# Three attentions of a 2,048-token block rebuilt: two float32r parts instead of three bf16 ones, scores and maxima on two halves of the rows, maxima over 1,024 keys, outputs kept by token, and the values weighed for two key tiles at a time

## The reference, cut to what is computed

```python
x = x + _L0_attn_a_ref(_layernorm(x), ...)        # token mixer
x = x + _L0_ffn_ref(_layernorm(x), ...)           # "F"
x = x + _L0_attn_b_ref(_layernorm(x), ...)        # "L", causal
x = x + _L0_ffn_ref(_layernorm(x), ...)           # "H", same weights as F

# inside _L0_ffn_ref: full attention, 16 heads of 8 channels
h = _layernorm(x, ln1_g, ln1_b)
q, k, v = h @ Wq, h @ Wk, h @ Wv                  # (1, 2048, 16, 8) each
scores = einsum('bqhd,bkhd->bhqk', q, k) / sqrt(8)
x = x + einsum('bhqk,bkhd->bqhd', softmax(scores), v) @ Wo
... layer norm, 8 experts, top 2 ...

# inside _L0_attn_b_ref: the same shape with a causal mask; the kernel
# multiplies the small latent matrices out first, so that q, k, v are
# again 2048 x 16 x 8 and no output projection is left
attn = where(causal, attn, -inf); attn = softmax(attn)
```

## Time and profile before

| | us |
|---|---|
| median of 3 runs | 3383.09 (3382.2 to 3384.76) |
| span of the profiled execution | 3382.5 |
| TensorE busy | 3032.9 (90%) |
| TensorE weight loads | 1205.9 (36%) |
| VectorE busy | 2225.2 (66%) |
| ScalarE busy | 1668.8 (49%) |
| GpSimd busy | 168.7 (5%) |
| mean granted TensorE clock, of full speed | 0.915 |

### The profile page before, as it was taken

One profiled execution on the slowest core, in us unless ns is written; L12 is line 12 of the kernel. 1 busy time (PEld: TensorE's weight loads), 2 busy tenths in 40 slices (PEclk: granted clock), 3 DMA queues, 4 the chain that ended last, 5 costly groups with the idle time before them and its releaser, 6 DMA issues. The chain is left out here.

```text
span 3382.5 us, 48839 instructions
## 1 busy us (share of the span) xinstructions
PE 3032.9 (90%) x14997; PEld 1205.9 (36%) x14997; DVE 2225.2 (66%) x4191; ACT 1668.8 (49%) x2007; POOL 168.7 (5%) x88
## 2 busy tenths in 40 slices
PE   6788859999999997997799999958999999998998
PEld 2787732222222223443233333322222222222443
DVE  5444459988889893223667666647989888894322
ACT  4212123666666665433255555531666666666333
POOL 1222220000000000001100000011000000000000
PEclk9888866999999997998699999975999999999899
DMA  1000010110011011120111111111010000110211
GB/s 37 1 0 0 0 61 11 29 29 19 27 29 29 17 30 32 69 69 12 59 32 39 30 30 41 30 32 59 15 30 29 29 19 28 29 29 21 76 56 31
DMA packets 75059, 105.46 MB, mean 31 GB/s; under 512 B 17334, under 2 KB 48016, under 8 KB 72433
## 3 DMA queue, kind: packets, MB, share of 16 engines
q1 hardware_dynamic: 71755, 100.97, 9.8%
q10 hardware_dynamic: 3104, 1.94, 0.2%
HBM read 68.72 MB, written 20.55 MB: 26 GB/s over the span
## 5 line engine op out<-in xcount | busy, mean ns | idle before, releaser
L466 DVE TENSOR_REDUCE Hmaxes<-Hm 128x1 f32<-128x512 f32 x1044 | 658.2, 685 | 95.6 <-PE Hm L392 95.0
L466 DVE TENSOR_REDUCE Fmaxes<-Fm 128x1 f32<-128x512 f32 x1044 | 658.1, 685 | 95.5 <-PE Fm L392 95.1
L447 ACT ACTIVATE Hprob<-Hs 128x1024 f32<-128x1024 f32 x512 | 498.5, 1021 | 242.3 <-PE Hs L357 240.7
L447 ACT ACTIVATE Fprob<-Fs 128x1024 f32<-128x1024 f32 x512 | 498.5, 1021 | 242.1 <-PE Fs L357 240.6
L466 DVE TENSOR_REDUCE Lmaxes<-Lm 128x1 f32<-128x512 f32 (+3 forms) x664 | 373.1, 605 | 179.0 <-PE Lm L392 105.3
L447 ACT ACTIVATE Lprob<-Ls 128x1024 f32<-128x1024 f32 (+7 forms) x384 | 293.1, 776 | 268.5 <-PE Ls L360 144.8
L392 PE MATMUL Hm<-Hka,Hqa 99*128 99x512 bf16 x1044 | 381.6, 404 | 27.4 <-DMA Hvh<-Hvstack 11.5
L392 PE MATMUL Fm<-Fka,Fqa 99*128 99x512 bf16 x1044 | 381.4, 404 | 26.8 <-DMA Fvh<-Fvstack 11.0
L357 PE MATMUL Fs<-Fqa,Fka 99*128 99x512 bf16 x1024 | 308.3, 385 | 1.6 <-ACT Fprob L447 1.2
L357 PE MATMUL Hs<-Hqa,Hka 99*128 99x512 bf16 x1024 | 308.2, 384 | 1.6 <-ACT Hprob L447 1.2
L374 PE MATMUL Ho<-Hprob,Hvh 128*32 128x512 f32 x2048 | 276.3, 612 | 0.6 <-ACT Hprob L447 0.6
(11 more groups left out here) (428 smaller groups left out, 2883.7 us busy)
## 6 DMA issues: line engine op xcount, KB each, us to landing
FEwb<-FE_weights SPq DMA_DIRECT2D x8, 1024.0 KB, 5.9
HEwb<-HE_weights SPq DMA_DIRECT2D x8, 1024.0 KB, 5.3
Fqa<-F_qparts SPq DMA_DIRECT2D x51, 96.0 KB
Fka<-F_kparts SPq DMA_DIRECT2D x51, 96.0 KB
Lqa<-L_qparts SPq DMA_DIRECT2D x51, 96.0 KB
Lka<-L_kparts SPq DMA_DIRECT2D x51, 96.0 KB
Hqa<-H_qparts SPq DMA_DIRECT2D x51, 96.0 KB
Hka<-H_kparts SPq DMA_DIRECT2D x51, 96.0 KB
```

Of the source, the lines that this page charges most:

```text
L447: nc.scalar.activation(prob[:, kt % PSLOTS, q0:q1], sps[SLOT_OF[kt, half]][:, q0 - half * 1024:1024], ACT.Exp, scale=SCALE).then_inc(expd, 1)
L466: nc.vector.reduce_max(maxes[:, qt, kb:kb + 1], src[:, 0:n], AX.X).then_inc(max_free, 1)
```

## The change

**Parts.** Queries and keys are split in two parts of float32r (`PARTS = 2`), with one copy and one subtraction. The combinations are now 4 x 8 = 32 rows, and two rows for the maximum (`KROWS = 34`). Each head's rows are loaded twice, at rows 0 to 33 for the scores and from row 64 on for the maxima (`LOW = 64`, 33 rows), so that the two kinds of product use different row halves of TensorE. Two slots instead of three.

**Maxima.** An item covers 1,024 keys: two matmuls into a pair of banks and one reduction. There are 32 a head in F and H and 24 in L, and two pairs of banks. In L the diagonal is masked by VectorE in the same operation (`tensor_tensor_reduce` with the constant `later`), and no longer by matmuls. Splitting the maxima and copying the head's values into place are on GpSimd (two instructions for the split, one for the values).

**Scores.** Each block of 512 columns has a bank of its own in a ring of three; its exponential follows at once, over 512 columns instead of 1,024. The ring also takes the turned maxima and the turned output. In L GpSimd zeroes the upper triangle of the diagonal 128x128 of the weights (`affine_select`), and blocks start at the first query of the tile.

**Weighing.** `weigh` is called after the scores of each even key tile, for the two tiles before it, one behind the other.

**The output.** TensorE transposes the copied bank in four pieces (`deliver`), ScalarE gathers it into `heads`, tokens on the partitions, and VectorE divides once for 15 heads and once for the last (`scale_heads`). The way through memory is gone. `project_tokens` transposes the result and projects it; L needs one addition (`add_tokens`).

**Loops.** TensorE, SP and GpSimd loop over two heads at a time (`Fori(1, 7)`), VectorE and ScalarE over one. The memory rows of zeros, the bf16 identity and the bf16 masks are gone. The rest of the program is not changed.

```diff
-PARTS = 3
-MROW = 96
+PARTS = 2
+MROW = PARTS * PARTS * DH
 KROWS = MROW + PARTS
+LOW = 64
+LROWS = MROW + 1
-SLOTS = 3
-MSLOTS = 3
-EARLY_FULL, EARLY_CAUSAL = 20, 24
+EARLY_FULL, EARLY_CAUSAL = 8, 9
+TURN_FULL, TURN_CAUSAL = 13, 11
...
-    MAXES = [(qt, kb, min(BANK, (qt + 1) * P - kb * BANK) if causal else BANK)
-             for qt in range(NT) for kb in range(NB) if not causal or kb * BANK <= qt * P]
+    MAXES = [(qt, half, min(2 * BANK, keys(qt) - 2 * BANK * half))
+             for qt in range(NT) for half in range(2) if keys(qt) > 2 * BANK * half]
...
-    cost = lambda j: 250 if j == "turn" else 60 + MAXES[j][2]
-    done = np.cumsum([cost(j) for _, j in stream])
+    stream = [(1, j) for j in range(EARLY, NM)] + [(2, j) for j in range(EARLY)]
+    done = np.cumsum([120 + MAXES[j][2] for _, j in stream])
...
+            sps = [ctx.enter_context(nc.psum_tensor(f"{name}s{i}", [P, BANK], F32)) for i in range(3)]
+            mps = [ctx.enter_context(nc.psum_tensor(f"{name}m{i}", [P, 2 * BANK], F32)) for i in range(2)]
+            ops = ctx.enter_context(nc.psum_tensor(name + "o", [P, BANK], F32))
...
+                        last = nc.tensor.matmul(mps[j % 2][:, n * BANK:n * BANK + w],
+                                                qa[LOW:LOW + LROWS, s, qt * P:(qt + 1) * P],
+                                                ka[LOW:LOW + LROWS, s, k0:k0 + w], start=True, stop=True)
...
+                        pe.wait_ge(expd, entry(h, kt, n) + 1)
+                        nc.tensor.matmul(seat(kt, n)[:, 0:q1 - q0], ka[0:KROWS, s, kt * P:(kt + 1) * P],
+                                         qa[0:KROWS, s, q0:q1], start=True, stop=True).then_inc(scored, 1)
...
+                            for k in range(high):
+                                for ahead, j, n in low[round(len(low) * k / high):round(len(low) * (k + 1) / high)]:
+                                    maxima(h + ahead, i + (u + ahead) // 2, (u + ahead) % 2, j, n)
+                                score(h, i, u, kt, k)
+                            for back in (2, 1):
+                                if kt % 2 == 0 and kt > 0:
+                                    weigh(h, u, kt - back)
+                                elif kt == 0 and not first:
+                                    weigh(h - 1, 1 - u, NT - back)
+                            if kt == OUT_AFTER:
+                                deliver(h, source=ident if first else None)
+                            if kt == TURN_AT:
+                                turn(turn_entry(h), TURN_SEAT, h + 2 if rest else h + 1)
...
+                            for n, (q0, q1) in enumerate(blocks(kt)):
+                                act.wait_ge(scored, entry(h, kt, n) + 1)
+                                nc.scalar.activation(prob[:, kt % PSLOTS, q0:q1], seat(kt, n)[:, 0:q1 - q0],
+                                                     ACT.Exp, scale=SCALE).then_inc(expd, 1)
...
+                            nc.vector.tensor_tensor_reduce(
+                                out=mps[j % 2][:, 0:width], in0=mps[j % 2][:, 0:width], in1=later[:, 2 * BANK - width:2 * BANK],
+                                scale=1.0, scalar=LEAST, op0=ALU.add, op1=ALU.max,
+                                accum_out=maxes[:, qt, half:half + 1]).then_inc(max_free, 1)
...
-            attention(nc, name, main, G["Wq"], G["Wk"], G["Wv"], consts, yT, causal=False)
-            project_add(nc, name + "O", yT, G["Wo"], n1, n1, consts)
+            attention(nc, name, main, G["Wq"], G["Wk"], G["Wv"], consts, n2, causal=False)
+            project_tokens(nc, name + "O", n2, yT, G["Wo"], n1, n1, consts)
```

More of the change, by code:

```diff
@@ L6 @@
 F32 = mybir.dt.float32
-BF16 = mybir.dt.bfloat16
+F32R = mybir.dt.float32r
 ALU = mybir.AluOpType
@@ L212, in first_query, with blocks @@
+    ident = consts["ident"]
+    qscr = nc.dram_tensor(name + "_qparts", (PARTS, P, T), F32, kind="Internal").ap()
+    kscr = nc.dram_tensor(name + "_kparts", (PARTS, P, T), F32, kind="Internal").ap()
+    EARLY = EARLY_CAUSAL if causal else EARLY_FULL
+    TURN_AT = TURN_CAUSAL if causal else TURN_FULL
     def first_query(kt):
         return kt * P if causal else 0
-    def halves(kt):
-        return [h for h in range(2) if (h + 1) * 1024 > first_query(kt)]
-    def blocks(kt, half):
+    def blocks(kt):
@@ L219, in blocks @@
         lo = first_query(kt)
-        return [(max(lo, b * BANK), (b + 1) * BANK) for b in (2 * half, 2 * half + 1) if (b + 1) * BANK > lo]
-    MAXES = [(qt, kb, min(BANK, (qt + 1) * P - kb * BANK) if causal else BANK)
-             for qt in range(NT) for kb in range(NB) if not causal or kb * BANK <= qt * P]
-    NM = len(MAXES)
-    NHALF = sum(len(halves(kt)) for kt in range(NT))
-    SLOT_OF = {}
-    for kt in range(NT):
-        for half in halves(kt):
-            SLOT_OF[kt, half] = len(SLOT_OF) % 2
@@ L231, in attention @@
-    AHEAD = np.cumsum([0] + [len(halves(kt)) for kt in range(NT)]).tolist()
-    BEFORE = 1
-    EARLY = EARLY_CAUSAL if causal else EARLY_FULL
-    ITEMS = NM + 1
-    stream = ([(1, j) for j in range(EARLY, NM)] + [(2, j) for j in range(BEFORE)] + [(1, "turn")]
-              + [(2, j) for j in range(BEFORE, EARLY)])
-    def count(h, j):
-        if j == "turn":
-            return h * ITEMS + NM + BEFORE + 2
-        if j >= BEFORE:
-            return h * ITEMS + j + 2
-        return h * ITEMS + j + (2 if isinstance(h, int) and h == 0 else 1)
@@ L251, in attention, with keys @@
[L251 to L253 removed]
+        return [(q0, min(q0 + BANK, T)) for q0 in range(lo, T, BANK)]
+    def keys(qt):
+        return (qt + 1) * P if causal else T
+    MAXES = [(qt, half, min(2 * BANK, keys(qt) - 2 * BANK * half))
+             for qt in range(NT) for half in range(2) if keys(qt) > 2 * BANK * half]
+    NM = len(MAXES)
@@ new lines, in attention, with entry, out_entry, turn_entry @@
+    AHEAD = np.cumsum([0] + [len(blocks(kt)) for kt in range(NT)]).tolist()
+    NE = AHEAD[NT] + 2
+    BEFORE = NB + 1
+    OUT_AFTER = 1
+    def entry(h, kt, n=0):
+        return BEFORE + h * NE + AHEAD[kt] + n + (kt > OUT_AFTER) + (kt > TURN_AT)
+    def out_entry(h):
+        return BEFORE + h * NE + AHEAD[OUT_AFTER + 1]
+    def turn_entry(h):
+        return BEFORE + h * NE + AHEAD[TURN_AT + 1] + 1
+    def slot_of(offset):
+        return offset % 3
+    stream = [(1, j) for j in range(EARLY, NM)] + [(2, j) for j in range(EARLY)]
@@ L1567, in build @@
             normalize(nc, "N4", x, n1, main, consts)
-            attention(nc, "L", main, wq, wk, wv, consts, yT, causal=True)
-        project_add(nc, "LO", yT, None, x, x, consts)
+            attention(nc, "L", main, wq, wk, wv, consts, n2, causal=True)
+        add_tokens(nc, "LO", n2, x)
         clear_semaphores(nc)
```

743 lines of the change are left out of this document (381 added, 362 removed).

## The result

The changed kernel takes 3856.38 us, median of 4 runs (3848.41 to 3886.29), against 3383.47 us before: 1.142 times as long, 95% interval 1.1375 to 1.1461. The forecast was 3714 us, with a range of 3235 to 3900. The profiled execution spans 3846.7 us, 464 more than before.

A forecast was written before the change was run, and what follows sets the result against it. TensorE was taken as the bound in F's heads. With a swinging clock, F and H at +147.5 us each and L at +36 gave +331 on 3382.5, a forecast of 3714 us, range 3235 to 3900.

The forecast's parts named there:

- rival 1: Whole kernel: faster, 3262 us, the clock staying at 2.4 GHz because row halves together or the 128-row weighing suffice; chance 0.35.
- two walks: Heads, two key tiles stepped through the engines: 5.5 us at the high clock, 8.2 at 1.2 GHz; the middle was taken.
- The share of the low level: Heads of the attentions: clock expected to swing, about 0.75 granted; a quarter to three quarters low gave 3487 to 3938 us.
- the loop turns: TensorE's loop in F's heads: 5 us a turn, two heads to a turn, 1.7 us a head, 45.1 becoming 46.8.
- The last head: F's last head, no maxima but the same long weighing: 43 us against 33 at high clock, 50 in the forecast.
- the token mixer's 64-row stream: Evidence from the profile before: 7.1 us of back-to-back 64-row matmuls stayed at 0.50, so few rows count as little work.
- Rival 3: Maxima and scores: the row halves don't overlap, clock high, 49.5 and 33.3 us a head, 3434 us; chance 0.05.
- rival 4: Maxima and scores: float32r takes two passes, clock high, 52.0 and 35.8 us a head, 3549 us; chance 0.04.
- Rival 2: Whole kernel: the clock stays low all through, 4162 us; chance 0.06.
- A maximum over 1,024: VectorE's reduction: 0.60 + 0.53 = 1.13 us; first head's maxima 46 against 51.1 us in F, -5 (L -7).
- Splitting: Stage ahead of the maxima: two parts instead of three, 22.5 us instead of 30.6, -8 in each attention.
- The way out of F: Behind F's heads, 18.3 us: loses the way through memory (about 10), gains 16 transposes, -1.5 us net.

## Why the prediction held, and where its sizes were off

**The clock.** The forecast was slower for a cause that none of the operation counts shows, few rows, and the clock did swing: the runs with rows of zeros, and the kernel before with rows taken away, show from both sides that rows count. But in F it is half of the cause. The prediction took the long weighing for a help to the clock, an argument for rival 1. In F's full heads, those with maxima beside their scores, from the first copy of the output to the fourteenth, the changed kernel and its three variants give this, mean granted clock and us from copy to copy:

| | 33 and 34 rows | 64 and 64 rows |
|---|---|---|
| two tiles to a weighing | 0.70, 61.0 | 1.00, 46.2 |
| one tile to a weighing | 1.00, 42.7 | 1.00, 42.7 |

The low clock in the changed kernel's F needs few rows and the long weighing together, and the change brought both. (With 34 rows one at a time, in the kernel before, the rows are enough.) The argument of the prediction would have made the clock swing with one tile to a weighing too, and in F it doesn't; to that extent the right call there was luck. Why the long piece hurts was not tested; between two of them lie twice as many few-row pairs, with waits. In L the pattern is another (0.69, 0.79; 0.50, 0.91), and there the long piece helps as long as the rows are few.

The size was a middle between two walks, and there it fell short. A head of F took 974.5 / 16 = 60.9 us against 57.2 on the mean of the forecast, one of L 40.7 against 39.5. The term of the sum that was mis-sized is this price of the heads: 56 us in F, some 52 in H and 19 in L, 127 of the 133 us between the forecast's 3713.5 and the profiled 3846.7. (The median of the runs lies another 10 us above that execution.) The share of the low level was not what was off. With half of the heads' work at 45.1 and half at 66.7 us a head, 60% of the time is at the low level (66.7 / 111.8), a clock of 0.70, and the trace has 0.69; the "about 0.75" of the prediction is half of the time and doesn't fit its own walks. The steps were dearer. Three in a row and one at the high level:

```profile
718.75:727.23 8.48, 8.22 (x33) 3.50 (x32) 4.70 (x4) 4.21 (x9) 0.00 (x0) 0.50 0.07 18
727.23:735.08 7.85, 7.82 (x38) 2.98 (x37) 4.70 (x6) 4.88 (x11) 0.29 (x1) 0.72 0.52 117
735.08:742.63 7.55, 6.87 (x33) 2.43 (x32) 4.68 (x5) 4.23 (x9) 0.00 (x0) 0.73 0.00 0
673.84:679.60 5.76, 5.08 (x33) 2.02 (x32) 4.65 (x5) 4.26 (x10) 0.00 (x0) 1.00 0.07 14
```

The ends are 5.76 and 8.48 us where the walks had 5.5 and 8.2, and steps in which the level changes are the most frequent (60 of the 112 in the first fourteen heads have 0.72 or 0.73) and cost 7.3 to 7.9, more than the 7.1 halfway between the ends. The last head took 55.5 us where 50 stood. One error worked the other way: the loop turns, 1.7 us a head, were not there (below).

**The row taken as evidence** was the token mixer's 64-row stream at 0.50. It was the right row for few rows one at a time, as the 64-row run of the kernel before shows; the kernel before has no long weighing, and so no row for one next to few rows.

**The walk at the high level.** The prediction had 5.5 us for two tiles and 45.1 us a head before loop turns, 46.8 with them. With 64 rows and F at 0.97 the trace has a weighing at 701.59 and the next at 707.35:

```profile
701.59 1.92 PE L310 MATMUL Fo<-Fprob,Fvh 128*32 128x512 f32 x16
...
703.78 0.39 PE L273 MATMUL Fm<-Fka,Fqa 64*128 64x512 f32 x1
703.78 0.39 PE L285 MATMUL Fs<-Fqa,Fka 64*128 64x512 f32 x1
704.01 0.39 PE L273 MATMUL Fm<-Fka,Fqa 64*128 64x512 f32 x1
704.01 0.39 PE L285 MATMUL Fs<-Fqa,Fka 64*128 64x512 f32 x1
...
707.35 1.07 PE L310 MATMUL Fo<-Fprob,Fvh 128*32 128x512 f32 x8
```

5.76 us, and 46.2 us a head. So each step was 0.26 too short, and the 1.7 us a head for the loop turns were not there: the 13 spacings within F that lie ahead of the last two are 45.9 to 46.3 us, with no long one at a turn. Why a loop over three heads cost 5 us a turn and one over two heads costs nothing was not tested.

**Rival 1** said 3262 us at a high clock. No run had that clock in L with two tiles to a weighing; F's part of it was borne out (752 us for the heads, 46.8 x 15 + 43 = 745 by the rival), and L's 32.5 us a head stands beside 36.5 at 0.79 and 32.7 (522.5 / 16) at 0.91 with one tile. **Rival 3** is refuted by the starts within 10 ns and by the pairs at 703.78 and 704.01 above, 0.23 us apart at the high level; **rival 4** by their records of 0.39 us: float32r takes one pass at these shapes. The Trainium skill (FP8 and Floating Point Precision, TensorE Precision Notes) says only that the reduced form reads the word truncated; the records agree with what the prediction took from it. **Rival 2**, all low, came true only in other kernels.

**A maximum over 1,024** was 1.13 us by the sum. VectorE's records are 1.22, and the second of two follows 1.14 us behind the first (two take 2.36), so the price itself was right. The forms of the maxima over F, and in L's heads the masked ones over 1,024 keys:

```profile
L494 DVE TENSOR_REDUCE Fmaxes<-Fm x512: 1211/1216/1226, 492.8 to 1440.1; 128x1 f32<-128x1024 f32 x171
```

```profile
L489 DVE CUSTOM_DVE_ANT_0 Lm<-Lm,Llater 128x1024 f32<-128x1024 f32 x29 | 36.0, 1241 | 20.3 <-PE Lm L271 20.3
L489 DVE DVE_READ_ACCUMULATOR2_ANT Lmaxes<- 128x1 f32 x233 | 33.0, 141 | 0.0
```

But the clock is low in the first head's stage (0.53), and VectorE waits 0.18 us for TensorE behind each two: (2.36 + 0.18) / 2 = 1.27 each, some 50 us for 40, so the 5 us saved there were 0.8. In L the masked maxima also cost a second record of 0.14 us each, which the prediction left out: its first maxima became 1.9 us slower instead of 7 faster.

**Outside the heads.** Splitting saves 5.7 and 6.7 us, not 8: VectorE's eight subtractions last 0.69 us each and from the third on follow each other in 0.86. The way out of F saves 7.1 us, not 1.5: with the result by token on the chip the 16 transposes and the projection fit in the 11.2 us, of which TensorE works 7.7. The prediction took back too much for them from the 10 us through memory. All that lies outside the heads, the start of the program with it, makes up 6 of the 133 us.

## What to carry to other kernels

Packing two small matmuls on two row halves, or using fewer rows by fewer parts, saves columns but also takes active rows away; read the granted clock of the stage, and if it falls, pad the contraction with rows of zeros, which cost no columns. Measure a long piece of other work between them both ways: here it hurt the clock in one attention and helped it in the other. Ask of such a stage not only whether it stays at the high level but whether it can get there out of the stage ahead of it. And when a long piece is moved in an in-order queue, follow every buffer whose filling it would cut in two.

## What the runs showed of the hardware

- Rows of zeros count as active rows: 34 and 33 rows padded to 64 and 64 moved F's heads from 0.69 to 0.97, and the time from 3856 to 3346 us.
- The rows of matmuls that run side by side add up in F: 48 + 48 and 64 + 33 gave the same 0.85. In L they gave 0.70 and 0.72, 646.7 and 631.0 us.
- Few rows are not enough by themselves: with 33 and 34 rows and one tile to a weighing, F's full heads ran at 1.00 (555.3 us for 13 of them), with two tiles at 0.70. With 34 rows one at a time (the kernel before) they were enough: 0.50.
- TensorE can be busy without gaps and stay at 1.2 GHz for whole stages: 1353 of 1355 us with 34 rows, 1346 of 1347 with 64, one matmul at a time.
- The same code can sit at either level. H, the same as F, had 0.86 over its heads in the run with one tile to a weighing, where F had 0.94. Its first head stayed low, out of the maxima stage, and from the third copy of its output to the fourteenth it ran at 1.00:

```profile
2456.00:2527.20 71.20, 70.47 (x272) 28.26 (x271) 41.57 (x37) 37.11 (x71) 0.42 (x2) 0.50 0.09 20
2638.50:3108.30 469.80, 469.75 (x2873) 172.06 (x2875) 416.85 (x364) 375.18 (x738) 7.83 (x33) 1.00 0.11 25
```

- In L, shorter weighings were worse as long as the rows were few (0.69 with two tiles, 0.50 with one) and better once they were 64 (0.79 and 0.91). What lifts the clock there was not tested by itself.
